# Mamba inside two sparse FFNs on one NeuronCore: the causal convolution's shifted taps go from VectorE to ScalarE and GpSimd

## The reference, cut to what matters

```python
x = x + 0.5 * ffn(layernorm(x));  x = x + mamba(layernorm(x));  x = x + 0.5 * ffn(layernorm(x))

# ffn: I = 2048; of each 4 neighbours of h only the 2 largest magnitudes are kept
h = silu(x @ w_gate) * (x @ w_up);  out = keep_2_of_4(h) @ w_down

# mamba: E = 1024, N = 16, DC = 4
skip = xn @ W_skip.T;  u = xn @ W_in.T
u = silu(causal_depthwise_conv(u, conv_w) + conv_b)   # u[t] = sum_k w[k] * u[t-3+k]
delta = softplus(u @ Wd1.T @ Wd2.T + bd2);  Bt = u @ WB.T;  Ct = u @ WC.T
h[t] = exp(delta[t] * A) * h[t-1] + delta[t] * u[t] * Bt[t];  y[t] = sum_n h[t] * Ct[t]
out = ((y + u * W_D) * silu(skip)) @ W_out.T
```

## Time and profile before

| | us |
|---|---|
| median of 3 runs | 3949.71 (3949.53 to 3950.27) |
| the profiled execution, its own time | 3949.53 |
| its span, first to last instruction | 3947.8 |
| PE busy | 3575.9 (91%) |
| VectorE busy | 3237.4 (82%) |
| GpSimd busy | 2606.4 (66%) |
| ScalarE busy | 1867.7 (47%) |
| mean granted TensorE clock | 0.958 |

### The profile page before, as it was taken

The page is one execution under the profiler, slowest core; times in us unless marked ns, Lnnn a source line. Parts: engine busy times, 40 slices in busy tenths (PEclk is TensorE's granted clock), DMA queues, the critical chain, the costliest instruction groups (busy, mean ns, idle before and its releaser), DMA issues. The chain is left out here.

```text
span 3947.8 us, 37932 instructions
## 1 busy us (share of the span) xinstructions
PE 3575.9 (91%) x11264; PEld 2065.6 (52%) x11264; DVE 3237.4 (82%) x3568; ACT 1867.7 (47%) x2472; POOL 2606.4 (66%) x2057
## 2 busy tenths in 40 slices
PE   7999889999999999899999998889897888687788
PEld 5655545555656455555555554545454444354455
DVE  3435988787899889988999899988998899999832
ACT  3223546546554554546554565456453654353310
POOL 0003876765787778777786878767877889888700
PEclk8999989999999999999999999999998999898899
DMA  6444454644756456455564555536554455444332
GB/s 229 152 139 145 147 168 152 217 155 142 226 158 197 139 176 223 131 182 168 184 202 144 186 183 197 161 121 200 184 162 145 136 167 190 134 142 154 110 126 90
DMA packets 233147, 647.63 MB, mean 164 GB/s; under 512 B 25968, under 2 KB 26224, under 8 KB 223216
## 3 DMA queue, kind: packets, MB, share of 16 engines
q1 hardware_dynamic: 159216, 510.95, 37.6%
q10 hardware_dynamic: 73728, 134.25, 12.8%
HBM read 579.57 MB, written 65.54 MB: 163 GB/s over the span
## 5 line engine op out<-in xcount | busy, mean ns | idle before, releaser
L1085 POOL TENSOR_TENSOR db<-du,Bb 128x512 f32<-128x512 f32 x1024 | 1334.8, 1304 | 986.1 <-DVE decay L968 628.9
L1096 POOL TENSOR_TENSOR y<-y,pr 128x512 f32<-128x512 f32 x1024 | 1351.5, 1320 | 133.4 <-DVE pr L978 133.3
L968 DVE TENSOR_TENSOR_SCAN decay<-decay,db 128x512 f32<-128x512 f32 x1024 | 1251.3, 1222 | 112.8 <-ACT decay L690 105.4
L690 ACT ACTIVATE decay<-delta,aneg 128x512 f32<-128x512 f32 x1024 | 702.5, 690 | 1296.9 <-DVE pr L978 1292.7
L523 PE MATMUL main<-zhi,wunit 128*128 128x512 f32 x2048 | 959.4, 468 | 37.4 <-DVE zlo L912 27.7
L582 PE MATMUL side<-h,wdown 128*128 128x512 f32 x2048 | 926.0, 596 | 10.8 <-DVE res_r L953 8.6
L525 PE MATMUL main<-zhi,wunit 128*128 128x512 f32 x2048 | 807.5, 394 | 0.0
L524 PE MATMUL main<-zlo,wunit 128*128 128x512 f32 x2048 | 807.3, 394 | 0.0
L978 DVE TENSOR_TENSOR pr<-decay,Cb 128x512 f32<-128x512 f32 x1024 | 702.5, 686 | 28.3
L582 PEld LDWEIGHTS side<-h,wdown 128*128 128x128 f32 x2048 | 389.8, 191 | 419.9 <-issue 389.9
L598 PE MATMUL side<-xm,wmam 128*128 128x512 f32 x1024 | 475.9, 611 | 36.1 <-DVE cv L999 27.2
(11 more groups left out here) (75 smaller groups left out, 2380.3 us busy)
## 6 DMA issues: line engine op xcount, KB each, us to landing
wunit<-hl_dram SPq DMA_DIRECT2D x480, 512.0 KB, 3.8
wdown<-down_w_dram SPq DMA_DIRECT2D x256, 256.0 KB, 2.9
Bb<-bc_dram ACTq DMA_DIRECT2D x256, 256.0 KB, 3.9
Cb<-bc_dram ACTq DMA_DIRECT2D x256, 256.0 KB, 5.1
wmam<-mam_w_dram SPq DMA_DIRECT2D x64, 512.0 KB, 4.0
hl_dram<-wunit SPq DMA_DIRECT2D x32, 512.0 KB, 2.9
skip_dram<-skb SPq DMA_DIRECT2D x64, 256.0 KB, 4.1
delta<-skip_dram SPq DMA_DIRECT2D x16, 1024.0 KB, 6.8
```

The lines of the kernel that those rows point to most:

```text
L690: nc.scalar.activation(decay[u % BANKS][:], delta[:, e, :], ACT.Exp, scale=aneg[:, e, n:n + 1]).then_inc(sem["decay_ready"], 1)
L968: nc.vector.tensor_tensor_scan(decay[u % BANKS][:], decay[u % BANKS][:], db[u % RING][:], 0.0, ALU.mult, ALU.add).then_inc(sem["state_read ...
L1085: nc.gpsimd.tensor_tensor(db[u % RING][:], du[:, e, :], Bb[m % ROWS][:], ALU.mult).then_inc(sem["input_ready"], 1)
L1096: nc.gpsimd.tensor_tensor(y[:, e, :], y[:, e, :], pr[u % RING][:], ALU.add).then_inc(sem["sum_ready"], 1)
```

## The change

The three shifted taps leave VectorE. ScalarE now makes all four products of a chunk from the bank, three into new tiles `tp0` to `tp2` and the fourth with the bias into `cv`, and the fourth frees the bank. GpSimd adds the three `tp` tiles to `cv`, each addition waiting for the one before it. For sequences 1 to 7 that stands behind the scan work of the tick that comes three after the product's own, for sequence 0 one after. There is one set of `tp` tiles, so `taps` of a chunk waits until GpSimd has finished the chunk before (`conv_ready`), and `silu_u` waits for `conv_ready` too. `place_units` no longer charges VectorE for `in`.

```diff
-        vector = {"mean": 2.3, "var": 6.5, "down": 0.6, "out": 0.7, "win": 0.6, "in": 2.1}
+        vector = {"mean": 2.3, "var": 6.5, "down": 0.6, "out": 0.7, "win": 0.6}
...
+        tp = [sb(f"tp{k}", [P, L]) for k in range(DC - 1)]
...
-            def first_tap(key):
+            def taps(key):
...
+                if KE * b + e:
+                    act.wait_ge(sem["conv_ready"], KE * b + e)
                 if b == 0 and e >= 2:
                     act.wait_ge(sem["u_ready"], e - 1)
-                tap = C_CW + e * DC + DC - 1
-                nc.scalar.activation(cv[e % 2][:], bank_of(key)[:], ACT.Identity, bias=small[:, C_CB + e:C_CB + e + 1],
-                                     scale=small[:, tap:tap + 1]).then_inc(sem["conv_begun"], 1)
+                for k in range(DC - 1):
+                    shift = DC - 1 - k
+                    nc.scalar.activation(tp[k][:, shift:], bank[:, 0:L - shift], ACT.Identity, scale=tap(k))
+                nc.scalar.activation(cv[e % 2][:], bank[:], ACT.Identity, bias=small[:, C_CB + e:C_CB + e + 1],
+                                     scale=tap(DC - 1)).then_inc(read_of(key), 1)
 
             def silu_u(b, e):
-                wait_read(act, ("in", b, e))
+                act.wait_ge(sem["conv_ready"], KE * b + e + 1)
...
-            def shifted_tap(key, k):
-
-                _, b, e = key
-                c, bank, shift = cv[e % 2], bank_of(key), DC - 1 - k
-                if k == 0:
-                    dve.wait_ge(sem["conv_begun"], KE * b + e + 1)
-                else:
-                    dve.wait_ge(sem["conv_step"], (DC - 2) * (KE * b + e) + k)
-                ins = nc.vector.scalar_tensor_tensor(c[:, shift:], bank[:, 0:L - shift], small[:, C_CW + e * DC + k:C_CW + e * DC + k + 1],
-                                                     c[:, shift:], ALU.mult, ALU.add)
-                ins.then_inc(read_of(key) if k == DC - 2 else sem["conv_step"], 1)
...
+            def convolve(b, e):
+
+                c = cv[e % 2]
+                wait_read(pool, ("in", b, e))
+                for k in range(DC - 1):
+                    shift = DC - 1 - k
+                    ins = nc.gpsimd.tensor_tensor(c[:, shift:], c[:, shift:], tp[k][:, shift:], ALU.add)
+                    if k < DC - 2:
+                        ins.then_inc(sem["conv_step"], 1)
+                        steps[0] += 1
+                        pool.wait_ge(sem["conv_step"], steps[0])
+                ins.then_inc(sem["conv_ready"], 1)
...
+                for b in range(B):
+                    back = 3 if b else 1
+                    for key in plan.jobs_at[tick - back] if tick >= back else []:
+                        if key[0] == "in" and key[1] == b:
+                            convolve(b, key[2])
```

More of the change, by code:

```diff
@@ L314, in build @@
             "decay_ready", "input_ready", "state_ready", "weighted_ready", "sum_ready",
-            "conv_begun", "conv_step", "u_ready",
+            "conv_step", "conv_ready", "u_ready",
             "first_term_ready", "du_ready", "gated_ready", "dve_step",
@@ L752, in root @@
                 nc.scalar.activation(rt, rt, ACT.Sqrt).then_inc(sem["root_ready"], 1)
-            def first_tap(key):
+            def taps(key):
                 _, b, e = key
+                bank = bank_of(key)
+                tap = lambda k: small[:, C_CW + e * DC + k:C_CW + e * DC + k + 1]
                 wait_job(act, key)
@@ L837, in _ @@
                     if key[0] == "in":
-                        first_tap(key)
+                        taps(key)
                     if key[0] == "skip":
@@ L1053, in _ @@
                 begin(share(units, 2, 4))
-                for key in jobs:
-                    if key[0] == "in":
-                        shifted_tap(key, 0)
                 if tick - 2 in plan.base:
@@ L1059, in _ @@
                     compare_with(plan.base.index(tick - 2), 1)
-                for key in jobs:
-                    if key[0] == "in":
-                        shifted_tap(key, 1)
                 finish(share(units, 2, 4))
                 begin(share(units, 3, 4))
-                for key in jobs:
-                    if key[0] == "in":
-                        shifted_tap(key, 2)
                 if tick - 2 in plan.base:
@@ L1074, in _ @@
         def _(pool):
+            steps = [0]
             def scan_input(u):
```

## The result

The changed kernel takes 3972.8 us (median of 4 runs, 3972.5 to 3977.2) against 3950.0 us for the kernel before (median of 4): a ratio of 1.0061, 95% interval 1.0048 to 1.0074. Faster by 25 us was forecast, and slower by 23 us came. The rival of a GpSimd for which all wait had 3977 us. The range held the time. Nine further executions of the changed kernel took 3969.5 to 3981.8 us, and the median of all thirteen is 3973.6 us. All times here are of executions in the chip's usual state; one of the kernel with extra additions took 6588 us at a granted clock of 0.747 and is left out.

The account below looks back on a forecast made before the run. PE was taken as the bound, with 170 us winnable in the eight half-scans with taps. The terms -30 - 13 - 17 + 36 = -24 us on 3949.5 us gave 3925 us; the range of 8 in 10 was 3888 to 3978.

Parts of the forecast that it names:

- The rival of a GpSimd for which all wait: Sequence 4's to 6's scans: comparisons held by additions, db late, ScalarE stopped in taps; 0.8 reaches PE, 3977 us, chance 0.27.
- What bounds the kernel: Eight half-scans with taps: PE idle 118.2 us and 51.5 us of lower clock, so at most 170 us to win.
- PE gets back 30 us of its waits for the taps: PE's 37.1 us of waits for taps, bank now freed earlier by ScalarE: eight tenths won, another 13 us by the clock.
- a lighter VectorE: Eight half-scans: VectorE loses 8% of its work; 15% of the remaining 81.1 us PE idle time won, 17 with clock.
- ScalarE's lead hides its products: Three more products, 2.1 to 2.3 us a chunk, hidden by a lead of one decay; if not, VectorE waits 22 us.
- Additions: length and number: GpSimd: three additions a chunk, 1.23 us each plus 0.1 us waits, 4.0 us a chunk, 224 us in eight windows.
- Comparisons held up by 55 us: In or just behind ticks with taps, 14 of 20 comparisons wait 4 us more for GpSimd's additions: 55 us of VectorE.
- One third of it reaches PE: Of 55 + 34 + 20 us of delays, one third costs PE time: 36 us.
- The three GpSimd terms: Comparisons held up 55 us, GpSimd falling behind its units 34 us, ScalarE waiting for additions 20 us.
- ScalarE waits for additions, 20 us: taps of a chunk waits for GpSimd's additions of the chunk before: ten waits of 2 us.
- Placement: Cost table moves 18 units into the ticks with taps; counted within the 12 us gain from VectorE's lighter work.
- Sequence 0: Without a scan, products and additions loop in 6.9 us a chunk, PE delivers every 6.87 us: nothing counted, 3 us possible.

Follow-up runs that it names:

- the kernel with extra additions: Kernel before plus three full GpSimd additions a chunk on tiles of their own, for which nobody waits: 3981.2 us, ratio 1.0077.
- short to full additions: Changed kernel with GpSimd's additions cut to one column each, 3915.9 us, against the changed kernel with full ones, 3973 us.
- Memsets: Kernel before plus GpSimd memsets of 1.3 us each in place of the three extra additions: 3970.6 us, ratio 1.0054.
- One gap a unit: Kernel before with one more GpSimd wait a unit, the addition into y waiting for the db of the same unit: 3939.2 us, ratio 0.9962.

## Why the prediction was wrong

The sum was 60 us of gains and 36 us of costs. The runs give a sum of the same form: 50 us for VectorE's relief, 15 us for the length of ScalarE's products, 57 us for the length of GpSimd's additions, or -50 + 15 + 57 = +22 us. The sign went wrong by the price of the additions and by the products, which had none.

- **What bounds the kernel.** Right: the half-scans with taps carry the loss (17 of the 23 us by the windows). Outside them 6 us were lost, forecast at nothing.
- **PE gets back 30 us of its waits for the taps (43 with the clock), and 12 us by a lighter VectorE (17).** As a ceiling this was near: all gains were 60 us and measured 50, with both products and additions short. PE then waits 9.1 us for the convolution instead of 38.6, so the 30 us were right there. In the changed kernel it waits 34.6 us: the same matmuls now wait for ScalarE. "PE waits on nothing of it directly" failed.
- **ScalarE's lead hides its products.** This failed. They had no term in the sum, only a share in the caution over the 12 us, and they cost 14 to 15 us. The waiting itself was foreseen: VectorE was to stop at the decay instead of at the product, 97.1 us, and 22 us more if the cover failed. Its wait for decays rose by 118 us. The price of those 22 us for PE was left out.
- **Additions: length and number.** Right: 1.27 us, gaps 0.08 us (0.1 assumed), three in 3.95 us (4.0), GpSimd at 87% (86%) of the eight stretches. The 0.5 us named for a wait on another engine is the idle time of such waits, the other engine's work included. In the trace of before the released instruction starts 0.03 to 0.10 us (medians by pair of engines) after the end of the one it waited for.
- **Comparisons held up by 55 us.** Mis-sized: the comparisons rose by 33 us. Another 20 us fell on norms, gates and `du`, which were not in the forecast, and the total of 53 us comes near to 55 by luck. VectorE also slipped in between additions, as the lower bound had it, but the following additions and comparisons then took turns.
- **One third of it reaches PE.** This failed, and with it the sign. The three GpSimd terms were 109 us of VectorE and ScalarE and 36 us of the time. The runs price them together at 57 us (short to full additions), about 0.52, or 30 us without the other changes. Against gains of 60 us these 57 would still have left it 3 us faster; with 50 and the products' 15 it is 22 us slower. The one comparison that cost PE nothing was a poor measure. Memsets, beside which comparisons run freely, still cost 20 us. The rival that expected a slower kernel named the right waits. Its number came of a share of 0.8 against gains of 60 us, where the runs show 0.52 against 50, and 15 us for the products.
- **ScalarE waits for additions, 20 us.** Mis-sized: 59.9 us in 20 waits. What it costs is not settled; with fewer such waits and more GpSimd work the kernel was slower.
- **Placement.** Counted as a gain, it won nothing that shows and may have cost about 7 us, because the new table says nothing of GpSimd.
- **Sequence 0.** Near: the first scan starts at 356.4 us instead of 358.9.
- **Signs.** PE idle 136 us in the eight stretches (under 100 forecast), comparisons 380 us (about 400), GpSimd busy 2896 us (near 2850).
- **The rule of the Trainium skill** ("SBUF — State Buffer", Who interferes with whom), a block of one instruction: the traces agree where GpSimd leaves a gap (1.1 us for each of the two later comparisons above), and show a longer block, up to 8.43 us, wherever GpSimd runs without one.

That the time lies in the range owes something to luck: its upper end was the rival's, and the forecast's own range ended at 3940 us.

## What to carry to other kernels

An engine's idle share is not room for new work when its runs hold up another engine. Look at what the other one does at the same time, and at the longest run without a gap. A wait that disappears at one instruction can stand at the next: add up who waits for whom over all lines before calling it won or new. The engine that takes over a piece can also take over the wait for it. Where a cost table places work, a moved piece needs its cost on the engine that now does it.

## Not expected of the hardware

- VectorE instructions with two SBUF inputs wait for a gap in GpSimd's run, not for the end of one instruction: 8.4 us through seven GpSimd instructions late in sequence 6's scan, and 25 of 25 held-up first comparisons of the kernel before begin at such a place. A gap of 0.08 us is enough to let them in, and with one in each unit the longest hold-up of a first comparison is 1.09 us.
- A GpSimd memset, which reads nothing, does not hold them up: beside it comparisons took their usual 1.21 and 0.68 us.
- One gap a unit wins 14 us and the second loses 30: 3939 us with one, 3969 us with two. Each adds 0.12 us to a unit of 2.46 us, on an engine that is busy 70% with them. The second shortens no hold-up and doubles VectorE's wait for `db` (26.6 to 56.5 us).
